# Router products of two batch rows strewn tile by tile between the last k tiles of attention, in a two-layer gated transformer kernel

## The reference

```python
x = x + tanh(g_xattn[0]) * L0_xattn(layernorm(x), ctx, ctx)   # 16 heads of 16, bias on q, k, v, o, distance bias
x = x + tanh(g_ffn[0])   * L0_ffn(layernorm(x))               # ternary weights, relu, width 1024
x = x + tanh(g_xattn[1]) * L1_xattn(layernorm(x), ctx, ctx)   # relu on q, k, v; no output projection
x = x + tanh(g_ffn[1])   * L1_ffn(layernorm(x))

# L1_ffn: one expert of four for each token
logits = x @ W_router                       # (2048, 256) @ (256, 4)
expert_idx = argmax(logits, axis=-1)
h = gelu(einsum('th,ehi->tei', x, W1) + b1) # only the chosen expert's row is kept
y = h[expert_idx] @ Wo + bo + x
y = layernorm(y) * gamma + beta
```

## Time and profile before

| | |
|---|---|
| median of 3 runs | 830.56 us (826.97, 830.56 and 832.30) |
| profiled execution, whole | 835.91 us |
| its span of instructions | 834.1 us |
| TensorE busy | 737.3 us (88%) |
| VectorE busy | 581.4 us (70%) |
| ScalarE busy | 440.8 us (53%) |
| GpSimd busy | 296.2 us (36%) |

### The profile page before, as it was taken

One profiled execution on the slowest core, in us unless ns is written; L12 is line 12 of the kernel. 1 busy time (PEld: TensorE's weight loads), 2 busy tenths in 40 slices (PEclk: granted clock), 3 DMA queues, 4 the chain that ended last, 5 costly groups with the idle time before them and its releaser, 6 DMA issues.

```text
span 834.1 us, 12041 instructions
## 1 busy us (share of the span) xinstructions
PE 737.3 (88%) x4096; PEld 428.6 (51%) x4096; DVE 581.4 (70%) x1126; ACT 440.8 (53%) x840; POOL 296.2 (36%) x348
## 2 busy tenths in 40 slices
PE   5897599999998998999768999899999886899991
PEld 3443234343432676777523334333353775799981
DVE  5473689999970489265758899799943537577775
ACT  2222488888887535665016888687853422233330
POOL 2121255555554234755000000755423304233322
PEclk9897699999999999999877999999975989899996
DMA  8497355454444431002722255522012202111100
GB/s 298 112 180 219 108 179 180 169 170 155 166 166 155 152 101 51 1 1 73 173 62 81 71 175 169 149 77 64 18 46 83 92 1 90 39 48 44 42 15 21
DMA packets 51357, 87.52 MB, mean 105 GB/s; under 512 B 8598, under 2 KB 16792, under 8 KB 51297
## 3 DMA queue, kind: packets, MB, share of 16 engines
q1 hardware_dynamic: 44320, 72.06, 28.2%
q0 software_dynamic: 4576, 11.54, 5.3%
q10 hardware_dynamic: 2400, 3.15, 1.1%
HBM read 45.29 MB, written 41.63 MB: 104 GB/s over the span
## 4 chain that ended last, share of the span: by engine, by line
PE 56%; issue 11%; DVE 11%; DMA 8%; POOL 6%; SPq 4%; ACT 3%; POOLq 0%; DVEq 0%; ACTq 0%
PE ps_out L712 14%; PE ps_a L698 10%; PE ps_wide L593 6%; DVE row_max L1395 5%; PE ps_misc L698 5%; PE ps_a L522 4%; DMA out_x<-sorted_rows,ids 3%; PE ps_a L830 3%; SPq L438 2%; PE ps_wide L688 2%; POOL sorted_rows L1287 2%; PE ps_wide L894 1%; POOL hid_lo L1255 1%; PE ps_out L844 1%; ACT probs L1020 1%
## 5 line engine op out<-in xcount | busy, mean ns | idle before, releaser
L1395 DVE TENSOR_REDUCE row_max<-ps_wide 128x2 f32<-128x1024 f32 x256 | 301.1, 1219 | 34.0 <-PE ps_wide L593 27.8
L1020 ACT ACTIVATE probs<-ps_a 128x512 f32<-128x512 f32 x342 | 191.5, 602 | 57.4 <-PE ps_a L698 49.4
L593 PE MATMUL ps_wide<-stack_k,stack_q 48*128 48x512 f32 x512 | 155.1, 472 | 15.2 <-DVE row_max L1395 11.0
L698 PE MATMUL ps_a<-stack_q,stack_k 62*128 62x512 f32 (+1 forms) x342 | 142.3, 467 | 13.1 <-ACT probs L1020 10.1
L712 PE MATMUL ps_out<-probs,vals 128*17 128x512 f32 x1024 | 142.2, 631 | 0.5 <-POOL probs L1214 0.5
L698 PEld LDWEIGHTS ps_a<-stack_q,stack_k 62*128 62x128 f32 (+1 forms) x342 | 61.9, 194 | 102.4 <-ACT probs L1020 69.3
L1020 ACT ACTIVATE probs<-ps_misc 128x512 f32<-128x512 f32 x170 | 102.4, 603 | 19.4 <-PE ps_misc L698 15.5
L1214 POOL TENSOR_TENSOR probs<-probs,fixes_sb 128x512 f32<-128x512 f32 x64 | 82.2, 1284 | 82.5 <-ACT probs L1020 82.5
L593 PEld LDWEIGHTS ps_wide<-stack_k,stack_q 48*128 48x128 f32 x512 | 63.0, 191 | 50.5 <-DVE row_max L1395 20.2
L698 PE MATMUL ps_misc<-stack_q,stack_k 62*128 62x512 f32 (+1 forms) x170 | 78.8, 463 | 2.9 <-ACT probs L1020 2.9
L1199 POOL TENSOR_SCALAR max_neg<-row_max 128x16 f32<-128x16 f32 x32 | 9.2, 289 | 158.5 <-DVE row_max L1395 137.3
(11 more groups left out here) (214 smaller groups left out, 1326.7 us busy)
## 6 DMA issues: line engine op xcount, KB each, us to landing
rows_sorted<-blank SPq DMA_DIRECT2D x17, 1040.0 KB, 5.0
planes_k<-planes SPq DMA_DIRECT2D x32, 256.0 KB, 3.8
planes_q<-planes SPq DMA_DIRECT2D x32, 256.0 KB, 3.5
stack_q<-planes_q SPq DMA_DIRECT2D x64, 128.0 KB, 2.8
stack_k<-planes_k SPq DMA_DIRECT2D x64, 128.0 KB, 2.8
w_raw<-in_L_W SPq DMA_DIRECT2D x6, 1024.0 KB, 5.1
stack_q<-planes_q SPq DMA_DIRECT2D x64, 64.0 KB, 2.7
stack_k<-planes_k SPq DMA_DIRECT2D x64, 64.0 KB, 2.6
```

The source lines that it names most:

```text
L593: mm(raw_slot(l, ("pair", g, p))[:, i * S:(i + 1) * S], stack_q[at, slot(g, c) + q * P:slot(g, c) + (q + 1) * P], stack_k[at, slot(g, c):s ...
L698: mm(score_slot(("tile", n))[:], stack_k[at, slot(g, c) + k * P:slot(g, c) + (k + 1) * P], stack_q[at, slot(g, c):slot(g, c) + S], start=T ...
L1020: do(probs[n % PROBS[l]][:, j, :], score_slot(("tile", n * HG + j))[:], ACT.Exp, scale=0.25).then_inc(exp_done, 1)
L1395: v.tensor_reduce(row_max[:, g % 2, :, p], raw_slot(l, ("pair", g, p))[:].rearrange("p (i k) -> p i k", i=2), AX, ALU.max).then_inc(sem(f" ...
```

## The change

No work is added or taken away. Only places in the queues move:

- **TensorE.** `route_logits` takes a list of token tiles. For batch row 0: tile 0 behind the scores of (G-2, 2), tile 1 behind its `weigh`, tile 2 in the middle of the scores of (G-2, 3), tile 3 behind them. `turn_n3(1)` moves from the middle of (G-2, 2) to behind `weigh` of (G-2, 3). `count(0)` moves to the middle of the scores of (G-1, 0). Batch row 1: tile 0 behind the scores of (G-1, 0), tile 1 behind its `weigh`, tile 2 in the middle of the scores of (G-1, 1), tile 3 behind them. `count(1)` and `total(0)` move from (G-1, 0) to behind `weigh` of (G-1, 2).
- **ScalarE.** The two copies of `rows1(0)` stand ahead of the first and of the second exponential of (G-2, 2). Those of `rows1(1)` stand there in (G-1, 0), no longer in (G-2, 3).
- **VectorE.** Three of the four `update3` of batch row 2 move ahead of `route(0)`; the fourth and `aggregate(3, 2)` move ahead of `route(1)`; `normalise(G-3)` moves between `route(1)` and `place(1)`; `normal(3, 2)` moves from ahead of `normalise(G-2)` and `normalise(G-1)` to behind both.
- **The wide banks** are taken in an order that fits this.

```diff
@@ raw_items
-                    for what, b in (("n3", 0), ("n3", 1), ("logits", 0), ("count", 0), ("logits", 1), ("count", 1)):
+                    for what, b in (("n3", 0), ("logits", 0), ("n3", 1), ("count", 0), ("logits", 1)):
                         yield (what, b)
+                if l == 1 and g == G + 2:
+                    yield ("count", 1)
@@ tensor: attention(l), inside for c in range(2)
                             scores(g, k, c, 1)
-                            if l == 1 and (g, k, c) == (G - 2, 2, 0):
-                                turn_n3(1)
+                            if l == 1 and (g, k, c) == (G - 2, 3, 0):
+                                route_logits(0, (2,))
+                            if l == 1 and (g, k, c) == (G - 1, 0, 0):
+                                count(0)
+                            if l == 1 and (g, k, c) == (G - 1, 1, 0):
+                                route_logits(1, (2,))
                         if l == 1 and (g, k) == (G - 2, 2):
-                            route_logits(0)
+                            route_logits(0, (0,))
                         if l == 1 and (g, k) == (G - 2, 3):
-                            count(0)
-                            route_logits(1)
+                            route_logits(0, (3,))
+                        if l == 1 and (g, k) == (G - 1, 0):
+                            route_logits(1, (0,))
+                        if l == 1 and (g, k) == (G - 1, 1):
+                            route_logits(1, (3,))
                         weigh(g * QT + k - BEHIND)
+                        if l == 1 and (g, k) == (G - 2, 2):
+                            route_logits(0, (1,))
+                        if l == 1 and (g, k) == (G - 2, 3):
+                            turn_n3(1)
                         if l == 1 and (g, k) == (G - 1, 0):
+                            route_logits(1, (1,))
+                        if l == 1 and (g, k) == (G - 1, 2):
                             count(1)
                             total(0)
@@ scalar: attention(l)
-                            if l == 1 and j == 0 and g == G - 2 and k - 2 in range(EARLY_ROWS):
-                                if k == 2:
-                                    act.wait_ge(sem("b1_split"), 1)
-                                rows1(k - 2)
+                            if l == 1 and (g, k, j) == (G - 2, 2, 0):
+                                act.wait_ge(sem("b1_split"), 1)
+                            if l == 1 and (g, k) == (G - 2, 2) and j < C:
+                                rows1(0, (j,))
+                            if l == 1 and (g, k) == (G - 1, 0) and j < C:
+                                rows1(1, (j,))
                             weights(g, k, j)
@@ vector: attention(l), behind the loop
                     normalise(G - 4)
+                    for t in tiles(2, None)[0:3]:
+                        update3(t)
                     route(0)
                     place(0)
-                    for t in tiles(2, None)[0:2]:
-                        update3(t)
+                    update3(tiles(2, None)[3])
+                    aggregate(3, 2, 1e-5)
                     route(1)
+                    normalise(G - 3)
                     place(1)
-                    for t in tiles(2, None)[2:4]:
-                        update3(t)
-                    normalise(G - 3)
-                    aggregate(3, 2, 1e-5)
                     tables(0)
-                    normal(3, 2, x)
                     normalise(G - 2)
                     normalise(G - 1)
+                    normal(3, 2, x)
```

More of the change, by code:

```diff
@@ L625, in turn_n3, with route_logits @@
                     last.then_inc(sem("turned_n3"), 1)
-            def route_logits(b):
-                slot_free("logits", b)
-                if b == 0:
-                    pe.wait_ge(sem("w_last"), 16 * 7)
-                pe.wait_ge(sem("x3_ready"), C * (b + 1))
-                for q in range(QT):
+            def route_logits(b, qs=range(QT)):
+                if qs[0] == 0:
+                    slot_free("logits", b)
+                    if b == 0:
+                        pe.wait_ge(sem("w_last"), 16 * 7)
+                    pe.wait_ge(sem("x3_ready"), C * (b + 1))
+                for q in qs:
                     for k in range(C):
@@ L636, in route_logits @@
                                   start=(k == 0), stop=(k == C - 1))
-                last.then_inc(sem("logits_done"), 1)
+                if qs[-1] == QT - 1:
+                    last.then_inc(sem("logits_done"), 1)
             def count(b):
@@ L987, in turned_out, with rows1 @@
                     do(xT[:, c, b * S:(b + 1) * S], spare_banks[c][:] if name == "n0" else wide(u), ACT.Copy).then_inc(sem(f"turned_read_{name}"), 1)
-            def rows1(b):
-                wait(act, sem("logits_done"), b)
-                for c in range(C):
+            def rows1(b, cs=range(C)):
+                if cs[0] == 0:
+                    wait(act, sem("logits_done"), b)
+                for c in cs:
                     act.wait_ge(sem("turned_n3"), b * C + c + 1)
```

## The result

The changed kernel takes 836.18 us (median of 14 runs, 832.62 to 842.31) against 830.93 us for the kernel before in the same series (14 runs, 826.97 to 836.04). The ratio is 1.0068, with a 95% interval of 1.0042 to 1.0095: slower by 3.5 to 7.9 us, so a real loss, though under one per cent. The forecast was a loss of 2.7 us.

A forecast was written before the change was run, and what follows sets the result against it. The prediction took TensorE as the bound, through its clock, halved for 30.7 us late in attention. Terms -0.5 + 0 + 2.2 + 1.0 gave +2.7 us on the 830.56 us median: 833.3 us, range 821 to 840.

The forecast's parts named there:

- the clock behind attention: Around turn_n3(2): TensorE's longer rest can drop the clock earlier, slowing transposes and router products; +1.0 us.
- Pieces of the router on TensorE: Last k tiles of attention: moved router pieces and counts cover waits for the first exponential; -0.5 us, bounds -1.0 and 0.
- When the clock falls: Last k tiles of attention: the clock falls again at about the same place, 616.1; 0 us, bounds -1 and +3.4.
- the third rival: Last k tiles of attention: clock falls one stretch earlier, 0.50 from 612.7; +7.7 to +9 us, 839 us; chance 0.15.
- `normal(3, 2)` behind the last `normalise`: VectorE, end of attention: it loses its idle-time cover and turn_n3(2) waits for it; +2.2 us, bounds 0 and 2.4.
- The rest, 0: Other moves on VectorE, ScalarE's copies and the wide banks: they fit in idle time and cost nothing.
- the clock would hold to the end of attention: Rival, last k tiles: strewing alone keeps the clock at 1.00; -9 us, 821.5 us; chance 0.15.
- it holds for a part: Rival, last k tiles: the clock falls at about 624, not 616; -5 us, 825.5 us; chance 0.10.

The follow-up runs named there:

- e1: The changed kernel with normal(3, 2) back in its old place on VectorE, ahead of normalise(G-2) and normalise(G-1): 835.77 us, ratio 1.0027.
- e5: e1 with roots(3, 2) on GpSimd moved ahead of the second set of scatters, place_rows(1): 833.95 us, ratio 1.0016 to the kernel before.
- e6: The changed kernel with eleven products of 512 columns behind the last turn_out, filling TensorE's rest ahead of turn_n3(2): 836.26 us, ratio 1.0044.
- e10: e5 with ten fp32r products of 512 columns added only in the tail, from attention's last product to the first block: 833.43 us, ratio 0.9980.
- e2: The kernel before with only normal(3, 2) moved behind normalise(G-1) on VectorE, nothing strewn: 837.47 us, ratio 1.0065.
- e11: The kernel before with ten fp32r products added only in the tail behind attention: 831.97 us, ratio 0.9957.
- e4: The kernel before with two fp32r products of 512 columns in each wait of attention's last k tiles, from (G-2, 3) on: 836.95 us, ratio 1.0017.
- e3: The changed kernel with two fp32r products of 512 columns in each wait of attention's last six k tiles: 843.75 us, ratio 1.0134.
- e9: e5 with ten plain float32 products of 512 columns in the last k tiles, plus the tail filling of e8: 833.79 us, ratio 0.9990.
- e8: e5 with all the filling of e7 and a few more such products in the tail behind attention: 839.91 us, ratio 1.0073.
- e7: The changed kernel with two fp32r products in each wait of the last k tiles, one behind each router piece, two behind each count: 845.69 us, ratio 1.0131.

## Why the prediction was right, and where its sum was off

The sign, the size class and the mechanism held: slower by less than one per cent, through a longer rest ahead of `turn_n3(2)` and a lower clock behind it. The sum was 2.7 us; the runs gave 5.25 us between the medians, with an interval of the ratio that begins at 3.5 us. So it was too small, and the term for the clock behind attention carries most of that.

To compare executions in which the clock fell at different places, I count work from n3(0) to n3(2) in full-clock time: the time at 1.00 plus half of the time at 0.50. (Waits for other engines don't shrink with the clock, so this is rough.) For the kernel before this is 608.59 to 648.92 with 30.7 us at half, so 9.6 + 15.35 = 25.0 us. For the changed kernel it is 604.90 to 644.54 with 3.4 + 20.5 = 23.9 us at half, so 15.7 + 11.95 = 27.7 us; less the 2.19 us that its rest is longer, 25.5 us.

1. *Pieces of the router on TensorE, -0.5.* The gain in waits is there: between n3(0) and n3(2) the profile has one wait of 0.45 us and four of 0.26 for an exponential before, and one and two after. But it is used up. Sixteen router products in a row take 1.88 us from their first start to the next instruction's (611.44 to 613.32); the four pieces of batch row 0 take 2.1 us together at the same clock, 0.50 to 0.54 each. With the rest taken off, the strewn orders without filling in the k tiles need 25.5 (changed kernel), 25.0 (e1), 25.5 (e5), 24.9 (e6) and 24.9 us (e10), the unstrewn ones 25.0 (before), 24.7 (e2) and 24.7 (e11). That is 25.2 against 24.8 on average, so strewing costs about 0.4 us of full-clock work, or up to 0.8 us at half clock. The term should have been about +0.5; its bounds ended at 0. The spread within the strewn group is as large as the difference, so even this is a weak finding.

2. *When the clock falls, 0.* Right for the first fall in this pair of profiles: 7.2 us behind n3(0) against 7.5. That the two agree so well is luck. In the other profiles without filling at that place the fall came 4.4 to 6.9 us behind n3(0), in both orders (e1, e5, e6 and e10 strewn; e2, e4 and e11 not). By the clock row alone the sign of the third rival, 0.50 in the stretch 612.7 to 616.1, was even there in the changed kernel; it came of the 3.7 us by which n3(0) itself was earlier. What the prediction did not foresee is that the clock may come back for a stretch. It did in the changed kernel, in e1, e3 and e5; without filling these had 23.9, 27.3 and 23.9 us at half clock, while e6 and e10, which share the strewn order, had 30.7 and 30.8 like the unstrewn kernels. The profiled execution of the changed kernel gained some 3.4 us by it, which hides most of the 4.9 us that it lost behind attention. For these two reasons, the early n3(0) and the returned clock, `turn_n3(2)` started at 644.54 and not near 651, as the prediction had it. Whether strewing makes this likelier can't be told from one profile of each.

3. *`normal(3, 2)` behind the last `normalise`, +2.2.* Right: the rest grew by 2.19 us. The prediction reasoned that `root` would be there in time, and it was (639.31 against 642.17). It left out the other side of that: with the late count, the old place of `normal(3, 2)` is no longer free either, since `root` comes late for it. e1 shows that price, 2.10 us of rest, and e5 shows that it needs a move on GpSimd to be free of both.

4. *The clock behind attention, +1.0.* This is the term that was off in size. Between the two profiles it measured 1.63 + 0.25 + 0.87 = 2.7 us. The bounds, 0 to 2.6 and 1.4 more, held it. Seven profiles whose queue behind attention has no filling show how the loss goes with the rest:

| kernel | rest ahead of `turn_n3(2)` | clock falls | time at 0.50 | n3(2) to n3(3) |
|---|---|---|---|---|
| e5 | 0.81 | 3.7 behind n3(2) | 6.8 | 12.56 |
| e4 | 0.81 | 3.2 behind | 6.8 | 12.56 |
| before | 0.85 | 4.7 behind | 3.4 | 11.30 |
| e1 | 2.10 | 2.1 behind | 10.2 | 14.16 |
| e3 | 2.98 | 1.3 ahead | 13.6 | 14.65 |
| e2 | 2.99 | 1.1 behind | 10.2 | 13.79 |
| changed | 3.04 | 1.6 behind | 10.2 | 14.03 |

All times are in us, one profile of each. With the short rests the piece takes 12.1 us on average, with the rests of about 3 us 14.2: the term is 2.0 us by these means, and 2.7 only against the kernel before, whose profile was the best of its kind. I took 1.0, nearer to nothing, because two rests of 0.85 and 0.80 us had left the clock at 1.00. The trace of the kernel before had a nearer row, which the prediction did not use, in front of the counting of batch row 2:

```profile
673.84 0.40 PE L646 MATMUL ps_wide<-running,sums_sb 128*128 128x16 f32 x2 [2.69 <-DVE onehot L1418]
```

```profile
674.20:681.00 6.80, 6.80 (x23) 5.75 (x23) 1.11 (x5) 0.60 (x1) 0.00 (x0) 0.50 0.01 2
```

A rest of 2.69 us ahead of thin products, and 6.8 us at half clock from 674.2 on. 6.8 us at half clock cost up to 3.4 us, and 3.4 us at half were there behind attention already, up to 1.7. So an estimate from this row would have been +1.7. The same rest stands in all thirteen profiles, and in each the clock fell between 0.6 us ahead of its end and 1.8 us behind it. That the loss comes with the rest alone, e2 shows, and e6 shows that most of it goes when the rest is filled.

5. *The rest, 0.* Right, with the reservation on GpSimd's queue under 3.

With the measured sizes the sum is +0.5 + 0 + 2.2 + 2.0 to 2.7 = +4.7 to +5.4 us, against 5.25 between the medians. That it agrees so closely is luck, given the interval of 3.5 to 7.9 and single profiles for the terms.

*The rivals.* That the clock would hold to the end of attention is refuted for this change: it fell at 612.1. e9 shows in addition what the prediction's arithmetic for it left open: a clock held by added work pays for itself and no more. That it holds for a part came true in another form, as the stretch 615.5 to 618.9. The page "TensorE: Matmul & The Clock Gate" of the Trainium skill, section "Why this matters for your kernels", advises to leave no idle gaps between bursts of matmuls. In the k tiles that did not suffice: e8 had no gap at all in 20.30 us, and its clock fell. Behind attention that advice and most runs agree: with the rests filled the clock stayed at 1.00 past n3(3) in e8, e10 and e11 (10.3 to 10.6 us from n3(2) to n3(3)), and in e6 past the router's products. e9 had the same filling there, and its clock fell at 654.8 all the same (11.5 us).

Open is what it is in the last k tiles that brings the clock down while TensorE is busy. The experiments show that plain float32 filling prevents most of it (e9). That fp32r filling puts the fall off is not shown: it came 5.8 us behind n3(0) in e3, 8.1 in e7 and 20.5 in e8. The experiments don't tell either whether it is the kind of product that matters, since no fp32r filling of the same total length was tried.

## What to carry to other kernels

Before a step is moved behind the last normalisation, look at which idle time it lies in now: its own duration is only the first half of the price, and the clock of what stands behind the longer rest is the other half. Size it from a rest of about that length elsewhere in the same trace. A rest that can't be removed behind a dense stage is worth filling with cheap wide products that write where nobody reads, for as long as the chain waits anyway (e11: 0.4% faster than the kernel before). Filling a stage in which TensorE is already the bound did not pay here: the products were paid for in full (e3, e7 and e8 slower, e9 the same).

## What the runs showed of the hardware

- The clock fell with TensorE busy for all of the 20.30 us before (e8, at 629.8). Idle time is not needed for a fall.
- Two executions with TensorE's work the same to within 0.05 us from 600 to 617.2 us parted: the clock fell at 617.4 in one (e7) and at 629.8 in the other (e8).
- A rest of 2.69 us ahead of the counting of batch row 2 stands in all thirteen profiles, and in each the clock fell within 1.8 us of its end.
- TensorE's code up to n3(0), the same in all the kernels, took between 604.9 and 611.4 us in single profiled executions. The time at 0.50 in it, 58 to 68 us, accounts for up to 5 us of that; the rest is not explained. Differences of 6 us between two profiles' spans say nothing about a change. Differences between two marks inside them say more, but they scatter too: 11.3 and 12.6 us for the same piece behind the same rest.
- One fp32r product of 512 columns between products of other shapes took 0.41 us (e7), and 0.25 us in a row of eleven (e6).
- The granted clock came back to 1.00 for a single stretch of 3.4 us in the middle of a long time at 0.50, without any change in how busy TensorE was (3.40 of 3.40 us in the stretch before it and in the stretch itself, in the changed kernel). e1, e3 and e5 have such a stretch too.
